# State-space heads: sum of squares taken once per batch, and state updates of a tile issued as a pair

## What is computed

```python
def step(state, inp):
    x_t, B_t, C_t, dA_t, dt_t = inp
    state = state * dA_t[..., None, None] + (dt_t[..., None] * x_t)[..., None] * B_t[:, :, None, None, :]
    y_t = jnp.einsum('bghps,bgs->bghp', state, C_t)
    return (state, y_t)
...
y = ys + D * x
g = y * silu(z)
g = g * rsqrt(mean(square(g), axis=-1) + EPS) * norm_w
out = g @ W_out
```

## Time and profile before

| | us |
|---|---|
| median of 3 runs | 1650.55 |
| lowest and highest | 1649.45, 1650.79 |
| the profiled execution, its own time | 1647.6 |
| span of its instructions | 1645.7 |
| the state-space heads in it | from 954.2 to 1300.6 |
| mean granted clock of PE | 0.895 of 2.4 GHz |

### The profile page before, as it was taken

One profiled execution on the slowest core, in us unless ns is written; L12 is line 12 of the kernel. 1 busy time (PEld: TensorE's weight loads), 2 busy tenths in 40 slices (PEclk: granted clock), 3 DMA queues, 4 the chain that ended last, 5 costly groups with the idle time before them and its releaser, 6 DMA issues. The chain is left out here.

```text
span 1645.7 us, 38779 instructions
## 1 busy us (share of the span) xinstructions
PE 1309.8 (80%) x13740; PEld 1003.8 (61%) x13741; DVE 1047.7 (64%) x2173; ACT 611.3 (37%) x1322; POOL 626.1 (38%) x556
## 2 busy tenths in 40 slices
PE   2798999988547999994356878988889539999992
PEld 1355666666436998993223446666667428989981
DVE  6488888978773555554685666666565464555554
ACT  2366676666423333331255721111111213333330
POOL 0254554455203333321003346666666212333320
PEclk9899999999758999997578959999999759999996
DMA  4556566564357111113100000000000257111115
GB/s 139 138 153 175 153 161 188 160 158 145 113 181 303 47 46 51 48 36 121 51 0 13 0 14 2 3 2 3 2 3 2 78 177 287 48 51 45 47 36 166
DMA packets 98815, 145.94 MB, mean 89 GB/s; under 512 B 32961, under 2 KB 76738, under 8 KB 96386
## 3 DMA queue, kind: packets, MB, share of 16 engines
q1 hardware_dynamic: 87746, 118.00, 24.0%
q0 software_dynamic: 8832, 24.13, 4.9%
q10 hardware_dynamic: 2112, 2.10, 0.4%
HBM read 87.57 MB, written 39.32 MB: 77 GB/s over the span
## 5 line engine op out<-in xcount | busy, mean ns | idle before, releaser
L1162 ACT ACTIVATE ffn_h<-ffn_bank,ffn_b 128x256 f32<-128x256 f32 x368 | 154.6, 471 | 323.0 <-PE ffn_bank L114 288.1
L1318 DVE CAST ffn_hh<-ffn_h 128x512 f16<-128x512 f32 x184 | 81.6, 443 | 204.7 <-ACT ffn_h L1162 192.2
L993 POOL DMA_INDIRECT ffn_xs<-xn_rows,ffn_from_rows x92 | 91.4, 994 | 307.5 <-PE ffn_bank L1070 201.3
L2108 POOL TENSOR_TENSOR ssm_GL<-ssm_L,ssml_G 128x512 f32<-128x512 f32 x128 | 165.0, 1298 | 111.5 <-DVE ssm_L L2017 111.4
L112 PE MATMUL ffn_bank<-ffn_hh,ffn_W 128*128 128x256 f16 x736 | 200.6, 273 | 3.8 <-DVE ffn_hl L1320 3.8
L113 PE MATMUL ffn_bank<-ffn_hl,ffn_W 128*128 128x256 f16 x736 | 200.6, 273 | 0.0
L114 PE MATMUL ffn_bank<-ffn_hh,ffn_W 128*128 128x256 f16 x736 | 200.6, 273 | 0.0
L1873 PE MATMUL ssm_Y<-ssm_GL,ssmh_windows 64*32 64x64 f32 x4096 | 148.4, 226 | 7.4 <-POOL ssm_GL L2108 7.0
L2017 DVE TENSOR_TENSOR_SCAN ssm_L<-ssm_bank,ssmh_ident 128x512 f32<-128x512 f32 x128 | 151.5, 1210 | 2.4 <-PE ssm_bank L1856 2.3
L1873 PEld LDWEIGHTS ssm_Y<-ssm_GL,ssmh_windows 64*32 64x32 f32 x4096 | 127.2, 112 | 37.1 <-issue 25.7
L1000 POOL DMA_INDIRECT y_rows<-ffn_y,ffn_to_rows x92 | 90.9, 989 | 143.1 <-DVE ffn_y L1328 129.1
(11 more groups left out here) (339 smaller groups left out, 3254.2 us busy)
## 6 DMA issues: line engine op xcount, KB each, us to landing
ffn_W<-split_w SPq DMA_DIRECT2D x16, 2048.0 KB, 13.6
att_piece<-in_ffn_w SPq DMA_DIRECT2D x32, 512.0 KB, 5.2
split_w<-att_halves SPq DMA_DIRECT2D x32, 512.0 KB, 4.3
att_Q<-att_pair SPq DMA_DIRECT2D x64, 128.0 KB, 2.4
ffn_back<-y_rows SPq DMA_DIRECT2D x16, 512.0 KB, 5.3
att_KB<-att_krl SPq DMA_DIRECT2D x8, 512.0 KB, 5.4
att_Q<-att_pair SPq DMA_DIRECT2D x64, 64.0 KB, 2.0
xn_rows<-ffn_XN SPq DMA_DIRECT2D x8, 512.0 KB, 3.1
```

The lines of the kernel that those rows point to most:

```text
L1162: ins_ = act.activation(h[layer][:, m, :], bank[1 + 2 * layer + u][:, (m % 2) * ST:(m % 2 + 1) * ST], ACT.Gelu, bias=bias[:, ds(e + m, 1)])
L2108: pool.tensor_tensor(GL[:, p % RING, :, :, :].rearrange("p x i n -> p x (i n)"), L[:, p % RING, :, :, :].rearrange("p x i n -> p x (i n)") ...
```

## The change

Squares. ACT squares the four blocks of a batch as before. DVE now adds blocks 1, 2 and 3 to block 0 in SBUF (`add_squares`, 128 x 512 float32, at the iteration where `read_squares` stood), and PE multiplies the sum by the ones once per batch, at the p of `outputs`, behind `multiply` and ahead of an update at the same p. ACT takes its root straight from PSUM bank 2. `ssum`, its clearing and `read_squares` are gone; `third_free` waits for the root (`sd_done`) in the place of `ss_read`.

Updates. A table entry is now a tile, not a chunk: PE issues the updates of both chunks of a tile one behind the other, the even chunk into bank 3 and the odd one into bank 2, at p = 0, 2, 4, 6 for batch 0 and at p = 32(b-1) + 17, 21, 25, 29 for the others; the last tile has the even chunk alone. `third_free` also waits for `state_done`. DVE fades the even chunk at p, takes it at p + 1, fades the odd one there, and takes that at p + 2. `weigh` of batches 1 to 3 moves with the table, one iteration later for the first tile (p = 32(b-1) + 15, 19, 23, 27).

```diff
--- before.py
+++ after.py
@@ -1789,7 +1789,7 @@
         norm_w, one_hot = sb("norm_w", [P, XB]), sb("one_hot", [P, SH])
         FTh, FTl = sb("FTh", [P, B // 2, S], F16), sb("FTl", [P, B // 2, S], F16)
         square, ones = zs, sb("ones", [P, 1])
-        ssum, sd, rstd = sb("ssum", [P, TB]), sb("sd", [P, TB]), sb("rstd", [P, TB])
+        sd, rstd = sb("sd", [P, TB]), sb("rstd", [P, TB])
         Y = ctx.enter_context(nc.psum_tensor("ssm_Y", [P, 4, 2, TB, CH], F32))
         bank = t.banks(4)
         bc_ready, scan_done, mult_done, window_done, y_done = (sem(n) for n in ("bc_ready", "scan_done", "mult_done",
@@ -1797,9 +1797,9 @@
         edtx_done, upd_psum, faded, state_done = (sem(n) for n in ("edtx_done", "upd_psum", "faded", "state_done"))
         decay_psum, decay_kept, inter_psum, inter_read, mixed = (sem(n) for n in ("decay_psum", "decay_kept", "inter_psum",
                                                                                   "inter_read", "mixed"))
-        y_read, gated, sq_done, ss_psum, ss_read = (sem(n) for n in ("y_read", "gated", "sq_done", "ss_psum", "ss_read"))
+        y_read, gated, sq_done, ss_psum, sq_summed = (sem(n) for n in ("y_read", "gated", "sq_done", "ss_psum", "sq_summed"))
         sd_done, rstd_done, out_psum, added = (sem(n) for n in ("sd_done", "rstd_done", "out_psum", "added"))
-        ones_done, sum_cleared, passed = sem("ones_done"), sem("sum_cleared"), sem("passed")
+        ones_done, passed = sem("ones_done"), sem("passed")
         loaded, hot_made, picks_made, more_picks = sem("loaded"), sem("hot_made"), sem("picks_made"), sem("more_picks")
         ident_made, cleared, eps_made, select_made = sem("ident_made"), sem("cleared"), sem("eps_made"), sem("select_made")
         ft_high, ft_low, wo_scaled = sem("ft_high"), sem("ft_low"), sem("wo_scaled")
@@ -1811,10 +1811,10 @@
         wide = lambda a: a.unsqueeze(2).broadcast_to([P, SH, SP_])
         flat = lambda a: a.rearrange("p x i n -> p (x i n)")
 
-        updates = {c: (0, c) for c in range(NC - 1)}
+        updates = {2 * i: (0, i) for i in range(TB)}
         inters = {8 + 2 * q: (0, q) for q in range(XB)}
         for b in range(1, B):
-            updates |= {PAIRS_B * (b - 1) + 16 + 2 * c: (b, c) for c in range(NC - 1)}
+            updates |= {PAIRS_B * (b - 1) + 17 + 4 * i: (b, i) for i in range(TB)}
             inters |= {PAIRS_B * b + 2 * q - 1: (b, q) for q in range(XB)}
         finishes = {PAIRS_B * b + at: (b, q) for b in range(B) for q, at in enumerate((19, 23, 40, 44) if b + 1 < B else (19, 23, 33, 34))}
         outputs = {PAIRS_B * b + (49 if b + 1 < B else 39): b for b in range(B)}
@@ -1834,7 +1834,8 @@
             def third_free():
 
                 pe.wait_ge(decay_kept, used["decay"])
-                pe.wait_ge(ss_read, used["squares"])
+                pe.wait_ge(sd_done, used["squares"])
+                pe.wait_ge(state_done, used["update"])
                 pe.wait_ge(added, used["output"])
 
             def fourth_free():
@@ -1874,13 +1875,16 @@
                                             GL[rows, p % RING, x, i, :], start=j % 4 == 0 and i == 0, stop=j % 4 == 3 and i == TB - 1)
                 ins.then_inc(y_done, 1)
 
-            def update(b, c):
-                i, par = divmod(c, 2)
+            def update(b, i):
                 pe.wait_ge(edtx_done, b * TB + i + 1)
                 fourth_free()
-                pe.matmul(bank[3][:, :], Bt[rows_of(par), b * TB + i, :], edtx[rows_of(par), (b * TB + i) % 2, :], start=True,
-                          stop=True).then_inc(upd_psum, 1)
-                used["update"] += 1
+                third_free()
+                for c in (2 * i, 2 * i + 1):
+                    if c < NC - 1:
+                        rows = rows_of(c % 2)
+                        pe.matmul(bank[3 - c % 2][:, :], Bt[rows, b * TB + i, :], edtx[rows, (b * TB + i) % 2, :], start=True,
+                                  stop=True).then_inc(upd_psum, 1)
+                        used["update"] += 1
 
             def carry(b, q):
                 third_free()
@@ -1899,12 +1903,12 @@
                 used["decay"] += 1
                 used["inter"] += 1
 
-            def sum_squares(b, q):
+            def sum_squares(b):
                 pe.wait_ge(ones_done, 1)
-                pe.wait_ge(sq_done, b * XB + q + 1)
+                pe.wait_ge(sq_summed, (b + 1) * (XB - 1))
                 third_free()
                 for i in range(TB):
-                    ins = pe.matmul(bank[2][:, i:i + 1], square[:, b * XB + q, i * P:(i + 1) * P], ones[:, :], start=True, stop=True)
+                    ins = pe.matmul(bank[2][:, i:i + 1], square[:, b * XB, i * P:(i + 1) * P], ones[:, :], start=True, stop=True)
                 ins.then_inc(ss_psum, 1)
                 used["squares"] += 1
 
@@ -1926,12 +1930,12 @@
                     spread(p + 2)
                 if 1 <= p <= NP:
                     multiply(p - 1)
+                if p in outputs:
+                    sum_squares(outputs[p])
                 if p in updates:
                     update(*updates[p])
                 if p in inters:
                     carry(*inters[p])
-                if p - 3 in finishes:
-                    sum_squares(*finishes[p - 3])
                 if p - 1 in outputs:
                     project(outputs[p - 1], 0)
                 if p - 3 in outputs:
@@ -1962,10 +1966,10 @@
 
             def root(b):
                 act.wait_ge(eps_made, 1)
-                act.wait_ge(ss_read, (b + 1) * XB)
+                act.wait_ge(ss_psum, b + 1)
                 if b:
                     act.wait_ge(rstd_done, b)
-                act.activation(sd[:, :], ssum[:, :], ACT.Sqrt, scale=1.0 / SD, bias=eps[:, :]).then_inc(sd_done, 1)
+                act.activation(sd[:, :], bank[2][:, 0:TB], ACT.Sqrt, scale=1.0 / SD, bias=eps[:, :]).then_inc(sd_done, 1)
 
             act.wait_ge(cleared, 1)
             window(0)
@@ -1997,7 +2001,6 @@
                                 identf[rows, rows].unsqueeze(1).broadcast_to([CH, 2 * TB, CH])).then_inc(ident_made, 1)
             dve.tensor_scalar(pick(4, SH // 4), hot(4, SH // 4), UNSCALE, None, ALU.mult).then_inc(picks_made, 1)
             dve.memset(ones[:, :], 1.0).then_inc(ones_done, 1)
-            dve.memset(ssum[:, :], 0.0).then_inc(sum_cleared, 1)
             dve.wait_ge(ident_made, 2)
 
             def split_decays():
@@ -2033,7 +2036,7 @@
                     dve.tensor_copy(states[:, 0, :], bank[3][:, :]).then_inc(state_done, 1)
                 else:
                     dve.wait_ge(faded, b * (NC - 2) + c)
-                    dve.tensor_tensor(states[:, c, :], states[:, c, :], bank[3][:, :], ALU.add).then_inc(state_done, 1)
+                    dve.tensor_tensor(states[:, c, :], states[:, c, :], bank[3 - c % 2][:, :], ALU.add).then_inc(state_done, 1)
 
             def read_inter(b, q):
                 n = b * XB + q
@@ -2050,19 +2053,18 @@
                 dve.tensor_tensor(block_g, Y[:, at:at + 2, q % 2, :, :].rearrange("p a i n -> p i a n"), block_g,
                                   ALU.add).then_inc(y_read, 1)
 
-            def read_squares(b, q):
-                n = b * XB + q
-                dve.wait_ge(ss_psum, n + 1)
-                dve.wait_ge(sum_cleared, b + 1)
-                if q:
-                    dve.wait_ge(ss_read, n)
-                dve.tensor_tensor(ssum[:, :], ssum[:, :], bank[2][:, 0:TB], ALU.add).then_inc(ss_read, 1)
+            def add_squares(b, q):
+                if q == 0:
+                    return
+                dve.wait_ge(sq_done, b * XB + q + 1)
+                if q >= 2:
+                    dve.wait_ge(sq_summed, b * (XB - 1) + q - 1)
+                dve.tensor_tensor(square[:, b * XB, :], square[:, b * XB, :], square[:, b * XB + q, :], ALU.add).then_inc(sq_summed, 1)
 
             def invert_root(b):
                 dve.wait_ge(sd_done, b + 1)
                 if b:
                     dve.wait_ge(added, 2 * b)
-                dve.memset(ssum[:, :], 0.0).then_inc(sum_cleared, 1)
                 dve.reciprocal(rstd[:, :], sd[:, :]).then_inc(rstd_done, 1)
 
             def add_output(b, half):
@@ -2081,16 +2083,23 @@
                     split_decays()
                 if p == 5:
                     scale_out_weights()
+                if p - 2 in updates and updates[p - 2][1] < TB - 1:
+                    b, i = updates[p - 2]
+                    take_update(b, 2 * i + 1)
+                if p in updates and updates[p][1]:
+                    b, i = updates[p]
+                    fade(b, 2 * i)
                 if p - 1 in updates:
-                    take_update(*updates[p - 1])
-                if p in updates and updates[p][1]:
-                    fade(*updates[p])
+                    b, i = updates[p - 1]
+                    take_update(b, 2 * i)
+                    if i < TB - 1:
+                        fade(b, 2 * i + 1)
```

(10 more changed lines are left out.)

## The result

The changed kernel is slower: its median is 1659.85 us, that of before in the same rounds 1648.65, ratio 1.0066 (95% interval 1.0045 to 1.0087). 1634.0 was forecast, with 1646.5 as the upper end. The profiled execution has a span of 1658.8 us.

What follows compares the result with a forecast made beforehand. PE waiting for DVE's scan was taken to bound later stretches, a 0.50 clock the first. Pipeline 8.0 + removed falls 4.9 - new fall 3.4 + early rise 7.1 = 16.6 us, giving a median of 1634.0, range 1628.5 to 1646.5.

Steps and rivals of the forecast that it cites:

- Paired updates: Loop of update, take, scan and spread: a pair takes 8.01 us where it took 8.74, gaining 0.73.
- The price of fade and add: DVE in the heads stage: a fade costs 0.58 us, and an add of 128 x 512 about 0.6.
- The output: From iteration 49 to 1127.2: costs 3.45 us, gains 3.5, net nothing; the first root's table load costs 1.3 more.
- Sum of the pipeline: Heads stage without clock effects: 2.1 + 0.9 + 5.2 - 1.3 + 2.1 - 1.0 = 8.0 us of gain.
- Clock after products with ones: Mid-stage: three clock falls vanish, gaining 4.9 us; one new fall at an output costs 3.4.
- Clock in the first stretch: Iterations 0 to 7: clock rises between 967 and 971 instead of 991, gaining 7.1 us, bounds 0 and 8.1.
- Between carries and output: Iterations 39 to 47: two products with ones go and POOL becomes the bound, gaining 2.6 us.
- The signs: Profile after: 32 products with ones, clock 1.00 before 975, scan wait below 35 us, iteration pairs of 8.0 us.
- The rivals: Whole kernel: late clock 1641.0 (0.32), gain eaten by DVE or POOL 1648.5 (0.09), low clock through outputs 1658.6 (0.05).
- low clock through the output: Rival at iterations 49, 81 and 113: clock stays low past the first projection, 7.0 us each, 1658.6; chance 0.05.

Runs made afterwards that it cites:

- serial_pair: The changed kernel with PE waiting for the first update of a pair before issuing the second: ratio 1.0032 to the kernel before, -5.6 us against the change.
- fade_hold: fade_later with hold's repeated spreads: ratio 0.9958 to the kernel before, -4.0 us against fade_later.
- hold: The changed kernel with spreads issued five times in the two iterations behind each pair in batches 1 to 3: ratio 1.0021 to the kernel before.
- take_later: product_later with DVE's take two iterations behind most single updates of batches 1 to 3 instead of one: ratio 0.9964 to the kernel before.
- fade_later: The changed kernel with the odd chunk's fade moved from behind the even take to behind the next scan: ratio 0.9982 to the kernel before.
- product_later: The kernel before with only the product with ones and the reading of its sums one iteration later: ratio 0.9971 to the kernel before.
- early_table: The changed kernel with a one-column Sqrt at the stage's start, to load the table early: ratio 1.0117 to the kernel before.
- fade_table: fade_later and early_table together: ratio 0.9982 to the kernel before, the same as fade_later.
- upd_fade_hold: upd_fade with repeated spreads in only the first iteration behind a pair: ratio 0.9902 to the kernel before, median 1632.67 us.
- upd_fade: The kernel before with paired updates, odd fades behind the next scan, one product with ones per block at p + 4, no adds: ratio 0.9934.

## Why the prediction was wrong, point by point

- *Paired updates*, "two updates and a plain iteration bring it to u + 3.45": wrong for PE, the pair takes 1.13 us. That took from PE work that kept the clock up; serial_pair gives it back and gains. On DVE the sum had the take at u + 1.16, the fade at 1.77 and the scan at 2.35. Measured are 1.16, 1.88 and 2.82: the take holds DVE for 0.72 (0.61) and the fade for 0.94 (0.58). These 0.47 us are the whole excess of the loop, 9.08 us from iteration 17 to 21 where 8.0 and 0.6 for a block reading were forecast. So a pair gained 0.3 us and not 0.73.
- *The price of fade and add*, 0.58 us "as its nearest row": the failed step. The row was of a fade that starts ahead of POOL's product. Behind a take it starts inside one, and waits. Fades measured 1.06 and adds 0.99 us on average. I had charged the collision to POOL alone (0.17 each, 1.0 in all); on DVE it came to 8.5 us for the fades and, against a fade of 0.67, to 3.9 for the adds. fade_hold against hold shows what the order weighs at an equal clock, length and place together: 10.4 us. take_later, with fades of 1.34 us, shows DVE filled by them.
- *The output*: the root's wait was 2.0 us with the table load (forecast 1.3 + 0.45) and 0.71 at the second output (0.45). The projection waited 1.06 us in iteration 50 and 2.11 in 82 (0.85 each).
- *Sum of the pipeline*, 8.0 us of gain: the largest miss. Held against before with the clock at 0.99 (hold), iterations 16 to 124 lost 4.2 us; with the 4.9 us that I had credited for the falls of before, which no run isolates, it is an estimated 9. At 1.00, hold's stretch 80 to 94 takes 45.5 us where 41.9 was the price of that work, and 16 to 30 takes 35.2 for 33.7. I had forecast nothing and a gain of 2 to 3. The known part of the miss is the price above, 12.4 us more on DVE; how much of it lies on the path isn't shown.
- *Clock after products with ones*: I forecast one new fall for 3.4 us. Seven came, 37.5 us long, and with all but 3.4 us of them gone (hold) the ratio falls by what is 7.4 us. Less the 4.9 of relief that is a loss of some 2.5, where a gain of 1.5 was forecast. Before, each of the three falls came some 1.0 us behind the start of a product. After, the products can't be what mattered: two of the seven falls come before the first product, and three more over 25 us behind the last one. PE's idle time goes with all seven, and hold and serial_pair, which change PE's work alone, take falls away. With the falls held off, the change still costs 3.5 us and not 10.9.
- *Clock in the first stretch*: right in the number's direction, not shown in the mechanism. The clock rose at 966.2 (forecast between 967 and 971), and 1 to 7 took 24.3 for 28.7 us; but it fell twice more before 990, so 4.4 us and not 7.1. In fade_later it was 8.2, but serial_pair, whose fades are in the old order, took 21.2 us, a gain of 7.5. And take_later has before's program here, with an update in each iteration from 0 to 6, and its clock also rose at 966.3: its iterations 1 to 7 took 26.0 us at a mean of 0.70, the same work that before did in 28.7 at 0.50. So dense updates don't hold the clock down by themselves. The two differ in the last fall ahead of the stage (at 953.6 in before, 942.4 in take_later); whether that decides the rise is open, and some of these gains may be luck.

```profile
959.40:985.40 26.00, 22.88 (x251) 12.71 (x250) 22.04 (x26) 2.49 (x7) 11.14 (x10) 0.70 0.01 1
```

- *Between carries and output*: right, 1.9 us for 2.6; but product_later shows that the late reading does it.
- *The signs*: the product has 32 records and POOL's products average 1.31 us, as said. PE's wait for the scan rose from 42.2 to 56.8 us where under 35 was named, and pairs take 9.1 us, not 8.0 and a reading.
- *The rivals*: low clock through the output was the nearest in its number (1658.6), by luck. The early rise that it left out came, no fall came at the third output, and five of the seven came away from the outputs.

Not settled: why a removed wait brings falls in other places (early_table, fade_table), what before the stage sets the clock of its first iterations, and so how much of a single run's time is chance of where the falls land.

## What to carry to other kernels

Price an instruction of VectorE with two SBUF inputs by what GpSimd does when it starts, not by its mean: here the same fade took 0.67 or 1.0 to 1.6 us, and its place in the order decided. Taking work from TensorE where VectorE is what it waits for can cost the clock for more than the work; look at PE's busy share ahead of each fall before counting it as a gain. Read a sum one iteration later before redesigning how it is made.

## What the runs showed of the hardware

Two float32 matmuls of 64 rows, on different row halves and into different banks, took 1.13 us together, where one took 1.12.

The fade that started 0.47 us ahead of the end of a product ended 0.55 us behind it, and so did, to 0.01 us, all 18 fades of the changed kernel that started inside an instruction of GpSimd, whether 0.5 or 1.1 us of it were left. The other way round, the product that started behind a fade with 0.30 us of it left took 1.43 for 1.27 us. The Trainium skill (SBUF — State Buffer, "Who interferes with whom") says that of a VectorE instruction with two SBUF inputs and a GpSimd instruction that reads SBUF the one that issues second waits; the rows agree, in both orders, with some 0.13 us of the second instruction going on beside the end of the first. In the prediction that rule stood with its cost on POOL alone; with the order of issue read from the timeline it would have put it on DVE.

Repeating matmuls that only write the same results again made the kernel faster: hold against the change by 7.4 us, and upd_fade_hold against upd_fade by some 5 (0.9902 and 0.9934, their intervals overlap).
